# A four-layer network on one core: the last pair's layers 2 and 3 in two sets of tokens, new orders of all steps, and unread products

## The reference

```python
# layer 0: attention with 16 heads and a mask, plus ctx @ Wg.T, then relu ffn
x = x + self_attn(ln(x), mask) + (ctx @ Wg.T + bg);  x = x + relu(ln(x) @ W1.T + b1) @ W2.T + b2
# layer 1: one head over ctx, gelu bottleneck of 4, then attention over itself
nX, nF = ln(ctx), ln(x);  cr = gelu(attn(nF, nX, nX) @ fc1.T + b) @ fc2.T + b
nc = ln(cr);  x = nF + gamma2 * (cr + gamma1 * attn(nc, nc, nc))
# layer 2: attention with 16 heads, causal, keys from ctx, then gelu ffn
x = ln(attn16(x, ctx, causal) + x);  x = gelu(x @ W1.T + b1) @ W2.T + b2 + x
# layer 3: attention with 8 heads, keys from ln(ctx), then a recurrence over the 128 tokens
x = x + attn8(ln(x), ln(ctx));  U = (ln(x) @ W_in.T + b_in) @ Bmat
s_t = silu(s_(t-1) @ A.T) + u_t                      # 64 states for each of 16 batches
out = x + s_t @ Cmat + mean(prog) @ W_prog.T + b_prog
```

## Time and profile before

| | |
|---|---|
| median of 3 runs | 861.58 us (861.24 to 863.72) |
| the profiled execution | 860.23 us, its span 858.4 us, mean granted clock 0.971 |
| PE busy | 776.8 us, 90% of the span |
| DVE, ACT, POOL busy | 546.0, 428.9, 336.5 us |
| first and last silu of the recurrence | 776.7 and 850.0 us |

### The profile page before, as it was taken

The page is one execution under the profiler, slowest core; times in us unless marked ns, Lnnn a source line. Parts: engine busy times, 40 slices in busy tenths (PEclk is TensorE's granted clock), DMA queues, the critical chain, the costliest instruction groups (busy, mean ns, idle before and its releaser), DMA issues.

```text
span 858.4 us, 17026 instructions
## 1 busy us (share of the span) xinstructions
PE 776.8 (90%) x5876; PEld 620.7 (72%) x5876; DVE 546.0 (64%) x2252; ACT 428.9 (50%) x1760; POOL 336.5 (39%) x344
## 2 busy tenths in 40 slices
PE   3798987899899989998999899988999978989997
...
DMA packets 16633, 21.42 MB, mean 25 GB/s; under 512 B 3869, under 2 KB 13090, under 8 KB 15906
## 3 DMA queue, kind: packets, MB, share of 16 engines
...
## 4 chain that ended last, share of the span: by engine, by line
PE 73%; DVE 17%; issue 4%; ACT 2%; POOL 2%; DMA 1%; SPq 0%; DVEq 0%
PE work_bank L601 23%; PE work_bank L592 21%; PE work_bank L730 6%; PE work_bank L652 4%; DVE probsT L1063 3%; DVE probs L966 3%; PE scores_bank L818 3%; PE work_bank L584 3%; PE scores_bank L562 3%; PE scores_bank L630 3%; PE work_bank L805 2%; DVE xn L984 2%; DVE stats L1003 2%; ACT probs L1162 2%; POOL probs L849 1%
## 5 line engine op out<-in xcount | busy, mean ns | idle before, releaser
L849 POOL TENSOR_TENSOR probs<-probs,rtotal 128x512 f32<-128x512 f32 x160 | 164.5, 1040 | 213.5 <-DVE rtotal L1053 213.3
L1162 ACT ACTIVATE probs<-probs,nmx 128x128 f32<-128x128 f32 x512 | 197.9, 390 | 74.6 <-DVE nmx L966 74.3
L1063 DVE COPY probsT<-work_bank 128x512 f32<-128x512 f32 x160 | 106.4, 680 | 17.7 <-PE work_bank L730 17.6
L601 PE MATMUL work_bank<-L_w,hidden 128*128 128x256 f32 x512 | 113.9, 381 | 0.0
L730 PE MATMUL work_bank<-ident,probs 128*128 128x128 f32 x640 | 97.5, 293 | 16.7 <-POOL probs L849 10.3
L849 POOL TENSOR_TENSOR rstd<-veps,half 128x2 f32<-128x2 f32 x64 | 45.4, 709 | 156.5 <-DVE veps L1011 155.8
L601 PEld LDWEIGHTS work_bank<-L_w,hidden 128*128 128x128 f32 x512 | 96.1, 190 | 14.0 <-ACT hidden L1217 1.7
L730 PEld LDWEIGHTS work_bank<-ident,probs 128*128 128x128 f32 x640 | 76.8, 149 | 36.2 <-POOL probs L849 17.4
L1162 ACT ACTIVATION_READ_ACCUMULATOR probs<-probs,nmx 128x1 f32 x512 | 97.0, 189 | 0.0
L584 PE MATMUL work_bank<-ident,xn 128*128 128x128 f32 x256 | 42.4, 289 | 21.1 <-DVE xn L984 21.0
L966 DVE CUSTOM_DVE_ANT_0 probs<-scores_bank,causal 128x128 f32<-128x128 f32 x256 | 57.1, 284 | 6.4 <-PE scores_bank L630 6.0
...
## 6 DMA issues: line engine op xcount, KB each, us to landing
...
```

Source lines behind the costliest of these rows:

```text
L601: mm = nc.tensor.matmul(d[:, b * D:b * D + D], xT, w, start=(n == 0), stop=(n == len(todo) - 1))
L849: return nc.gpsimd.tensor_tensor(out, a0, a1, op)
L1063: nc.vector.tensor_copy(turn_slot(s, i, key), d[:].rearrange("p (j k) -> p j k", j=4))\
L1162: ins = nc.scalar.activation(e_at[slot][:, j, :], src, ACT.Exp, bias=nmx[:, slot, j:j + 1], scale=1.0 if s == "C" else -1.0, accum_out=tot ...
```

## The change

All four orders and LOAD_ORDER are new. For layers 2 and 3 the last pair exists twice: B7, C7 with tokens 0 to 63 of both batches, and B8, C8 with tokens 64 to 127. `M7.self` writes its result so that a half of both batches fills 128 partitions; a projection of a half has 128 columns instead of 256, a layer 3 quad of a half has two tiles instead of four. Scores and mixes of a half are cut by batch (64 queries each):

```diff
+def blocks(s, i):
+    return (i - (NT - 1),) if s in "BC" and i >= NT - 1 else tuple(range(PAIR))
+def halved(s, i):
+    return len(blocks(s, i)) == 1
 ...
+                if halved(s, i):
+                    for c in range(DC):
+                        for b in range(PAIR):
+                            rows_of = slice(HALF * b, HALF * b + HALF)
+                            at = P * blocks(s, i)[0] + HALF * b
+                            for g in range(4):
+                                of = slice(32 * g, 32 * g + 32)
+                                keys = (k3T[of, c, b * P:b * P + P] if s == "C"
+                                        else kT["B"][of, c, b].rearrange("p e t -> p (e t)"))
+                                n = keys.shape[1]
+                                mm = nc.tensor.matmul(s_bank[g][rows_of, c * n:c * n + n], qT[s][of, c, at:at + HALF],
+                                                      keys, start=True, stop=True)
```

The half sums of layer 3 are written to `A_cur` and moved to `x7_all` by four DMAs of SP, in front of the four that fill `late`. The states of the recurrence move from `probs` to the memory of layer 0's W1, so it can begin while C8 still uses `probs`. It begins in front of `C8.turn.0`, and 21 of its steps stand among the steps of C8:

```diff
+STEPS_BEFORE = {("C", 8, ("turn", 0)): 9, ("C", 8, ("turn", 1)): 1, ("C", 8, ("turn", 3)): 1,
+            ("C", 8, ("turn", 2)): 1, ("C", 8, ("mix",)): 1, ("C", 8, ("out",)): 1, ("C", 8, ("flip", "x7")): 5,
+            ("C", 8, ("drive",)): 2}
 ...
+            def scan_step():
+                nonlocal scanned, part
+                t = scanned + 1
+                if t == 1:
+                    ready(exped, EXPED["C", NT, ("exp", 3)])
+                    for at in emptied_last([("C", j, ("drive",)) for j in range(NT)]):
+                        ready(*at)
+                    mm = from_u(0)
+                else:
+                    pe.wait_ge(silued, t - 1)
+                    mm = nc.tensor.matmul(s_bank[t // 32][0:SS, (t % 32) * B:(t % 32) * B + B], a_t[:],
+                                          w_state[:, t - 1, :], start=False, stop=True, skip_group_check=True)
+                mm.then_inc(stepped, 1)
+                scanned = t
+                if t in (8, 40, 72):
+                    if t == 40:
+                        ready(*done("C", NT, "drive"))
+                    from_u(t // 32 + 1)
+                elif t < FIRST_FROM:
+                    occupy(s_bank[3], 1)
```

The filler of a step has 128 columns where it had 144 (`occupy(s_bank[3], 1, P + 16)`). OCCUPIED is replaced; it names 38 steps with 149 unread products of 128 columns in place of 59 in front of ten:

```diff
+OCCUPIED = {("H", 0, ("flip", "x")): 20, ("H", 0, ("k",)): 6, ("H", 0, ("q",)): 3, ("A", 0, ("turn", 1)): 3,
+            ("A", 0, ("turn", 2)): 7, ("J", 0, ("v",)): 2, ("A", 0, ("mix", 1)): 3, ("A", 1, ("mix", 0)): 2,
+            ("A", 1, ("turn", 5)): 2, ("M", 0, ("turn", "a")): 1, ("M", 0, ("cross",)): 1,
+            ("M", 1, ("flip", "x3")): 7, ("B", 0, ("turn", 6)): 2, ("B", 0, ("mix", 1)): 1, ("J", 2, ("v",)): 1,
+            ("B", 2, ("turn", 1)): 5, ("G", 3, ("v1",)): 3, ("M", 4, ("flip", "x3")): 3,
+            ("A", 5, ("ffn1", 1)): 1, ("B", 4, ("flip", "o")): 3, ("A", 7, ("turn", 3)): 3,
+            ("M", 6, ("flip", "x3")): 2, ("A", 7, ("mix", 1)): 1, ("M", 7, ("flip", "x3")): 5,
+            ("B", 6, ("mix", 1)): 6, ("B", 6, ("flip", "o")): 1, ("B", 6, ("ffn1", 0)): 2,
+            ("B", 7, ("flip", "x4")): 7, ("C", 6, ("turn", 0)): 8, ("C", 6, ("turn", 1)): 2,
+            ("C", 6, ("turn", 3)): 5, ("B", 7, ("flip", "o")): 3, ("B", 7, ("flip", "x5")): 5,
+            ("B", 8, ("ffn1", 0)): 7, ("C", 7, ("turn", 1)): 2, ("C", 8, ("flip", "x6")): 3,
+            ("C", 7, ("flip", "x7")): 8, ("C", 7, ("drive",)): 3}
```

Of the orders, those parts that the prediction speaks of. PE, start, pair 3 in the middle, and the end:

```diff
-H0.flip.x G0.flip.cn H0.k H0.v H0.q A0.score.0 G0.v1 A0.score.1 A0.turn.0 A0.turn.1 A0.turn.2 A0.turn.3 A0.turn.4
-A0.mix.0 K0.k A0.turn.5 A0.turn.6 A0.turn.7 J0.k H1.flip.x J0.v A0.mix.1 H1.k A0.out H1.v H1.q K0.v A0.flip.x2
+H0.flip.x H0.k H0.q A0.score.0 H0.v A0.score.1 A0.turn.0 A0.turn.1 A0.turn.2 A0.turn.3 J0.v A0.turn.4 A0.mix.0
+A0.turn.5 A0.turn.7 H1.flip.x A0.turn.6 A0.mix.1 H1.k A0.out G0.flip.cn H1.v H1.q G0.v1 A0.flip.x2 A1.score.0
 ...
-A4.score.1 A4.mix.0 B2.turn.2 B2.turn.3 M3.flip.x3 B2.turn.4 B2.turn.5 B2.mix.0 B2.turn.6 M3.score.a B2.turn.7
+M3.flip.x3 G3.v1 B2.turn.4 B2.mix.0 B2.turn.5 M3.score.a B2.turn.6 B2.turn.7 C1.score J3.k A4.turn.4 B2.mix.1
 ...
-B6.ffn2 M7.turn.s C5.drive M7.self K6.v B7.flip.x4 C6.flip.x6 B7.q C6.q B7.score.0 B7.score.1 B7.turn.0 B7.turn.1
-B7.turn.2 B7.turn.3 C6.score B7.mix.0 K7.k B7.turn.4 B7.turn.5 B7.turn.6 B7.turn.7 C6.turn.0 C6.turn.1 B7.mix.1
-C6.turn.2 B7.flip.o C6.turn.3 C6.mix K7.v B7.flip.x5 C6.out B7.ffn1.2 B7.ffn1.3 B7.ffn1.0 C6.flip.x7 B7.ffn1.1
-C6.drive B7.ffn2 C7.flip.x6 C7.q C7.score C7.turn.0 C7.turn.1 C7.turn.2 C7.turn.3 C7.mix C7.out C7.flip.x7 C7.drive
+M7.flip.cr C5.out M7.score.s B6.ffn2 C5.flip.x7 J7.k M7.turn.s C5.drive M7.self B7.flip.x4 C6.flip.x6 K6.v C6.q B7.q
+B8.flip.x4 C6.score J7.v C6.turn.0 B7.score.0 C6.turn.1 C6.turn.3 B8.q C6.turn.2 K7.k B7.turn.1 B7.turn.0 C6.mix
+B8.score.0 B7.turn.2 B7.turn.3 C6.out B7.mix.0 B7.flip.o K7.v B7.flip.x5 B8.turn.0 B8.turn.1 B8.turn.2 B7.ffn1.2
+B7.ffn1.0 B8.turn.3 B7.ffn1.3 C6.flip.x7 B7.ffn1.1 B8.mix.0 C6.drive B8.flip.o B7.ffn2 B8.flip.x5 B8.ffn1.0
+C7.flip.x6 B8.ffn1.3 B8.ffn1.2 C7.q B8.ffn1.1 C7.score B8.ffn2 C7.turn.1 C7.turn.0 C7.turn.2 C7.turn.3 C8.flip.x6
+C7.mix C8.q C7.out C8.score C7.flip.x7 C7.drive C8.turn.0 C8.turn.1 C8.turn.3 C8.turn.2 C8.mix C8.out C8.flip.x7
+C8.drive
```

DVE, ACT and POOL around pair 3, and POOL's end:

```diff
-B2.turn.3 M3.flip.x3 B2.turn.5 A4.max.4 B2.turn.6 B2.mix.0 B2.turn.4 A4.max.5 A4.rec.4 A4.max.6 M3.max.a B2.turn.7
+A4.mix.0 B2.turn.3 A4.max.5 B2.rec.7 B2.rec.6 M3.flip.x3 A4.max.6 B2.turn.4 A4.rec.4 B2.mix.0 A4.rec.5 A4.max.7
+M3.norm.cr A4.stat.x2 C1.mix M3.flip.cr A4.norm.x2 G4.stat.c A4.flip.x2 A5.max.0 G4.norm.c C1.out A5.max.1 A5.max.2
 ...
-M3.mix.a B2.ffn1.2 B2.ffn1.3 B2.ffn1.0 B2.ffn1.1 C1.exp.0 C1.exp.1 C1.exp.2 C1.exp.3 M3.cross H5.k K2.v G4.flip.cn
+C1.exp.1 C1.exp.2 K2.k M3.mix.a C1.exp.3 M3.cross B2.ffn1.0 B2.ffn1.3 B2.ffn1.1 H5.q B2.ffn1.2 H5.k A5.exp.0 K2.v
 ...
-B2.nrm.6 A4.xb M3.rstd.x3 B2.nrm.7 M3.x3b A4.nrm.4 A4.nrm.5 M3.nrm.a H5.rstd.x A4.nrm.6 A4.nrm.7 B2.rstd.x5 B2.x5b
+C1.nrm.0 C1.nrm.2 M3.rstd.cr M3.x3b B2.x5b M3.crg A4.rstd.x2 M3.skip G4.rstd.c A4.x2b M3.nrm.s C1.rstd.x7 A5.nrm.0
 ...
+B7.x5b B8.rstd.x5 C7.rstd.x6 B8.x5b C7.nrm.0 C7.x6b C7.nrm.1 C7.nrm.2 C7.nrm.3 C8.rstd.x6 C7.rstd.x7 C8.nrm.2 C8.x6b
+C8.nrm.1 C7.x7b C6.x7b C8.nrm.3 C8.nrm.0 C8.rstd.x7 C4.x7b C8.x7b C3.x7b C5.x7b
```

More of the change, by code:

```diff
@@ new lines @@
+C1.turn.1 B2.ffn1.0 A4.out C1.turn.0 B2.ffn1.3 C1.turn.2 C1.turn.3 B2.ffn1.1 H5.q C1.mix M3.flip.cr B2.ffn1.2 H5.k
+A4.flip.x2 K2.v M3.score.s A5.score.0 C1.out B2.ffn2 M3.turn.s G4.flip.cn M3.self H5.v B3.flip.x4 A4.ffn1.3
+C1.flip.x7 B3.q C1.drive A5.turn.0 B3.score.0 G4.v1 A4.ffn1.2 A5.turn.1 A4.ffn1.0 A4.ffn1.1 A5.turn.2 A5.turn.3
+B3.score.1 C2.flip.x6 B3.turn.0 B3.turn.1 A4.ffn2 A5.score.1 B3.turn.3 B3.turn.2 A5.mix.0 C2.q B3.turn.4 M4.flip.x3
+B3.mix.0 B3.turn.5 B3.turn.6 M4.score.a B3.turn.7 C2.score A5.turn.4 J4.k A5.turn.5 B3.mix.1 K3.k B3.flip.o
@@ new lines @@
+M4.turn.a H6.flip.x A5.turn.7 M4.mix.a A5.turn.6 J4.v M4.cross A5.mix.1 C2.turn.0 B3.flip.x5 C2.turn.1 A5.out
+B3.ffn1.2 C2.turn.2 H6.k C2.turn.3 B3.ffn1.3 B3.ffn1.0 M4.flip.cr H6.q H6.v A6.score.0 C2.mix B3.ffn1.1 M4.score.s
+C2.out A5.flip.x2 K3.v B3.ffn2 M4.turn.s A5.ffn1.3 M4.self A5.ffn1.0 B4.flip.x4 C2.flip.x7 A5.ffn1.2 B4.q A6.turn.2
+C2.drive B4.score.0 A6.turn.0 A6.turn.1 G5.flip.cn A5.ffn1.1 B4.score.1 C3.flip.x6 B4.turn.0 A6.turn.3 B4.turn.1
+A5.ffn2 A6.score.1 A6.mix.0 B4.turn.2 B4.turn.3 C3.q G5.v1 B4.turn.4 M5.flip.x3 B4.mix.0 B4.turn.5 B4.turn.7
@@ L165 @@
-C7.turn.2 C7.turn.3 C7.mix C7.out C7.stat.x7 C7.norm.x7 C7.flip.x7 C7.drive
+H0.stat.x H0.norm.x G0.bias G0.stat.c H0.flip.x A0.max.0 A0.max.1 A0.max.2 A0.max.3 A0.rec.0 G0.norm.c H0.v A0.rec.1
+A0.max.4 A0.max.5 A0.max.6 A0.rec.3 A0.rec.2 H1.stat.x A0.turn.0 A0.max.7 A0.turn.1 A0.rec.5 A0.rec.4 A0.turn.3
+A0.rec.6 A0.turn.2 H1.norm.x A0.rec.7 J0.v A0.turn.4 G1.bias A0.mix.0 A0.turn.5 A0.turn.7 A0.turn.6 H1.flip.x
+A0.mix.1 A0.out A0.stat.x2 H1.v A0.norm.x2 A0.flip.x2 A1.max.0 A1.max.1 A0.ffn1.0 A1.max.2 A1.rec.0 A1.max.3
@@ new lines @@
+A1.rec.1 A0.ffn1.2 A0.ffn1.1 A1.rec.2 A0.ffn1.3 A1.max.4 A1.max.5 A1.rec.3 A1.turn.1 A1.max.6 A1.turn.2 A1.turn.0
+A1.max.7 A1.rec.6 A1.rec.4 A1.rec.7 A0.ffn2 M0.stat.x3 A1.turn.3 M0.norm.x3 A1.rec.5 A1.turn.4 A1.mix.0 M0.flip.x3
+H2.stat.x A1.turn.5 M0.max.a A1.turn.6 A1.turn.7 M0.rec.a H2.norm.x M0.turn.a G1.stat.c A1.mix.1 H2.flip.x
+M0.stat.cr G1.norm.c G2.bias A1.out A1.stat.x2 M0.norm.cr A1.norm.x2 M0.flip.cr A1.flip.x2 A2.max.0 M0.max.s
+A2.max.1 M0.rec.s A2.max.2 A2.rec.0 H2.v A2.max.3 A1.ffn1.3 M0.turn.s A1.ffn1.0 A1.ffn1.2 A2.rec.1 A2.max.4 M0.self
@@ new lines @@
+B3.mix.1 H6.norm.x C2.max.2 B3.flip.o M4.turn.a H6.flip.x B3.stat.x5 A5.turn.7 A5.turn.6 C2.rec.0 C2.rec.1
+B3.norm.x5 J4.v A5.mix.1 G6.bias C2.turn.0 C2.max.3 C2.rec.2 B3.flip.x5 M4.stat.cr C2.turn.1 C2.rec.3 A5.out
+C2.turn.2 A5.stat.x2 M4.norm.cr A5.norm.x2 C2.turn.3 M4.flip.cr C2.mix H6.v A6.max.0 M4.max.s A6.max.1 A6.max.2
+A6.max.3 A5.flip.x2 C2.out C2.stat.x7 G5.stat.c A6.rec.3 M4.rec.s M4.turn.s C2.norm.x7 B3.ffn2 A5.ffn1.3 M4.self
```

(1 more changed line is left out.)

520 lines of the change are left out of this document (269 added, 251 removed).

## The result

The changed kernel takes 0.964 of the time of the kernel before, interval 0.958 to 0.971 (run after run on the same chip, before: 861.41 us, median of 4). The profiled execution took 829.77 us, span 828.0.

What follows compares the result with a forecast made beforehand. TensorE, busy 90% of the span, was taken as the bound, losing time to idle, lower clock and a serial tail. 860.2 - 14.8 + 2.5 - 11 - 9 = 828 us; forecast 815 to 841 (0.48), range 806 to 857.

Steps and rivals of the forecast that it cites:

- a. The tail: Last pair as two token sets, one half's work filling the other's waits: -14.8 us, bounds -17.3 and -5.0.
- b. The recurrence: Recurrence starts before half 8 is ready, 21 steps among its last operations: +2.5 us in sum.
- 0.2 us of stall: Among half 8's last operations in the recurrence: steps would wait only 0.2 us for operations not ready.
- The filler's -1.5: Recurrence's first 66 steps: unread product of 128 instead of 144 columns saves 1.5 us, bounds 0 and 1.6.
- c. The order: New order of all steps from 8.4 to 690 us cuts idle and clock loss: middle -11, start -9 us.
- The earlier trace: Middle: M steps' scores wait five times for a copy of probabilities, 10.8 us; all goes, 8 counted as kept.
- d. The tables: ScalarE: 31 gelu/exponential switches against 23, 10.3 us more, hidden by its idle half; +10.3 if uncovered.
- 1: Rival, whole kernel: tail works, order doesn't, VectorE binds; 848 us, at most 858; chance 0.25 with mixtures.
- 2: Rival, whole kernel: nearly all TensorE idle goes; 807 us; chance 0.14 (below 815).
- 3: Rival, in-order queues: new waits at 2.5 us a place make it slower, 873 us at ten; 0.09 with Rival 4.
- 5: Rival, recurrence start: half 8's chain stops steps at every operation, 8 instead of 2.5 us, 834; inside forecast range.
- Rival 4: Recurrence: clock falls as its filler shrinks, +0.3 us a step, +38, 866 us; chance 0.09 together with 3.

Runs made afterwards that it cites:

- tail_alone: Kernel before's order of steps and loads, with the changed kernel's last pair in two token sets and its 53 unread products; 852.47 us, ratio 0.9882.
- order_alone: Kernel before with the changed kernel's step order and its 96 early unread products, last pair's layers 2 and 3 as one set; 846.25 us, ratio 0.9803.
- before128: Kernel before with 128 instead of 144 columns in the unread product behind recurrence steps 1 to 66; 860.41 us, ratio 0.9987.
- early_bare: respaced without the 96 unread products that stand before 690 us; 824.46 us, ratio 0.9575.
- respaced: Changed kernel plus three unread products before the recurrence, half 8's last operations reordered, 24 instead of 21 steps among them; 826.71 us, ratio 0.9619.

## Why the prediction was right, point by point

The forecast, 828 us, is 1.8 us from the profiled execution. The direction and the parts were right: both parts of the change win, as tail_alone and order_alone show. The closeness is luck: errors of 1.5 to 3.3 us cancel, inside the terms too, and the first stage alone moves by several us from trace to trace. In order, predicted and measured, from the trace:

- *a. The tail*, -14.8 against -17.3 (86.4 to 71.0 us, and 1.9 for J7.v's old place). Within it four sizes were wrong. The scores and mixes of halves were to add 4.0 us of work and add next to nothing: two halves of layer 2 take 2 x 1.12 us where the whole pair takes 2 x 1.15, and in layer 3 two halves take 2 x 0.70 where the pair takes 1.17. The clock is 1.00 instead of 0.94, so all of the 4.3 us came where two were taken. Against that PE idles 5.0 us beside the unread products, twice the 2.5 taken, and the unread products fill 13.6 us, not 12.3. The mechanism, one half's work in the other's waits, is right.
- *b. The recurrence*, +2.5 against +4.0. "0.2 us of stall" was the step that failed: the trace has 1.5 us, 0.63 from VectorE's order and 0.84 from a collision of VectorE with GpSimd's 1.26 us addition; the prediction had followed such additions in GpSimd's queue alone ("it just fits"). The rest is C8's work, some 4.2 us instead of 3.85. The filler's -1.5 was right for the steps: before128 against before, 71.6 us instead of 73.3. Of it only 0.7 us reach before128's median, since its trace has 9.9 us behind the last silu, the kernel before 8.4.
- *c. The order*, -20 against -16.7: start -9 against -6.2, middle -11 against -12.4 (of which 1.9 are J7.v). The earlier trace rows went and nothing of its size came in its place. In early_bare, which has the new order without unread products, the middle idles 17.2 us where the kernel before idles 28.4: 11.2 us are the order's, and the unread products take 1.0 back; predicted were 8 and 3 together, and no run splits them. The start's -6.2 is one trace against one, and by the spread given above -9 isn't refuted. What failed there is a reason: the unread products were to buy clock, and without them the time is no longer.
- *d. The tables*: 32 loads of 1.283 us against 24, 10.3 us more on ScalarE. PE never waits for `h` in 200 to 670 us; its one wait for `hidden` (0.9 us) is for VectorE, which comes to it late from its own queue. Hidden, as said.
- Behind the last silu 8.0 instead of 8.4 us. The sum: -17.3 + 4.0 - 16.7 - 0.4 = -30.4, from a span of 858.4 to one of 828.0.
- Two slips that the sum doesn't feel: 60 unread products lie before 200 us and 36 behind, not 61 and 35, and 0.01 x 462 us is 4.6 us of lost clock, not 2.5 (the fourth stage's clock is 0.993 with one digit more, 3.2 us).

Of the rivals, 1 is refuted by order_alone; 2 (807 us) stays out of reach, with respaced at 826.7 (its sum calls -14.8 a lower bound, which is a's middle value, a's bound being -17.3, and leaves b out); 3 wasn't seen: no wait of PE of 2 us is left in 200 to 670 us; 5 was a matter of degree, two waits in place of one at "every operation". Rival 4 held in half of the changed kernel's executions, at its predicted time, and is the prediction's real gap: the mechanism was there, with the reason against it that "the period of 0.551 is measured with 128 columns". That row was read late in the recurrence, where the steps run undisturbed and the clock is held; the change put C8's operations and their waits among the first steps, and nothing in the prediction asks what such a wait does to the clock. A forecast of one time for a kernel with two is right only by half. With the chance at 0.09 for rivals 3 and 4 together it was underrated.

On the clock the prediction set the Trainium skill ("TensorE: Matmul & The Clock Gate", What's actually happening), by which activity releases the slow state, against the rows: by that rule the unread products buy back all of the 12.5 us at the start. No run agrees. In the profiled execution the clock of 12.6 to 40 us rose from 0.75 to 0.95, but 40 to 200 us has 0.94 where it had 0.95, and its lost time, worked out as the prediction does, is still some 10 us. The eight traces with these products have 0.94 to 0.98 in 40 to 200 us, early_bare without them 0.97, and in 12.6 to 40 us the new order alone brings 0.87.
